# New instruction orders for all five engines of a two-layer attention kernel, weights requested by ScalarE, eight warm-up pairs

## Chip, core and metric

The kernel runs on one core of a Trainium2 chip. The metric is the device time of one execution in microseconds (us), as the median of several runs.

## What is computed

Two attention layers, one after the other, on x of shape (4, 128, 32, 32): four images, 128 channels, N = 1024 pixels. In each layer, for each image:

```
q = Wq x + bq     k = Wk x + bk     (16 x 1024 each)
v = Wv x + bv                       (128 x 1024)
energy = q^T k                      (1024 x 1024)
attn = softmax(energy, over keys)
x = gamma * (v attn^T) + x          (128 x 1024)
```

Everything is float32. Layer 1 works on the result of layer 0.

## The kernel before

There are eight stages, s = 0 to 7: stage s is layer s // 4 of image s % 4. Stages overlap. Each engine has its own instruction stream, and that stream is written out by hand: `PE_ORDER`, `ACT_ORDER`, `DVE_ORDER`, `POOL_ORDER` and `SP_ORDER` (lines 51 to 113) are lists of words such as `lo.6.3`: a kind of work, the stage, an index k or a half, and for TensorE's words a fourth number, the PSUM ring tile used. No planner runs; a program reads the words and emits the instructions, and semaphores are derived from the orders. Each engine takes its words strictly in order, so a word that waits holds all words behind it.

The kinds of work:

- `E` (TensorE): an energy tile, 128 queries by 1024 keys, into one of three ring tiles (two PSUM banks each). `max` (VectorE, line 563) takes its row maximum, `sum` (ScalarE, line 472) exponentiates and sums it. `log` (ScalarE) and `parts` (GpSimd, lines 391 to 396) turn maxima and sums into a shift for each query, in a high and a low part.
- `shift` (TensorE), `rows` (VectorE, line 572) and `place` (SyncE) put the shift into spare rows of the q and k operands.
- `ET` (TensorE): the transposed energies with the shift already in them. `attn` (ScalarE, line 484) exponentiates them into the SBUF tile attn.
- `hi` and `lo`: attn is split into a rounded high part (`hi`, line 359 on GpSimd, 490 on ScalarE) and the rest (`lo`: attn minus attn_hi, two SBUF inputs, line 364 on GpSimd, 558 on VectorE), so that TensorE can multiply both in its quick float32r mode. Of eight tiles of a stage, k = 1 to 6 are split; k = 0 and 7 are multiplied in plain float32. `v_hi` (370 on GpSimd, 495 on ScalarE) and `v_lo` (376 on GpSimd, 553 on VectorE) do the same for v.
- `PH` multiplies attn_hi by v_hi and v_lo (four passes), `PV` multiplies attn_lo by v_hi (two passes) or, for k = 0 and 7, the plain tiles. `finish` (VectorE, 581 and 586) forms gamma * out + x; `store` (SyncE) writes it out.
- `QX`, `QK` project q and k; `mask` and `stack` (VectorE, or GpSimd for stage 1 after `evac` on ScalarE) place them; `swap` (SyncE, line 323) copies the halves crosswise by DMA. `VX`, `V` and `v32` (line 548) make v. `raw` projects stage 0.
- `warm` is a number of matmul pairs on zeros; `WARM_UP` such pairs run first of all (lines 756, 757).

What holds buffers: `attn.s.k` may be written only when `lo.(s-1).k` has read the slot (for k = 0, 7: when `PV` has). `hi.s.k` needs the earlier stage's `PV` of that k. A ring tile is free when its reader is done. In the last two stages `PH` of each half of the output also waits for the `finish` of the same half of the stage before.

At the start SyncE issues, in this order, the DMAs of weights, of the two halves of image 0, of image 1, of `late` (v weights and layer 1), of units, and of images 2 and 3. ScalarE begins with the load of its activation table. The first `E` needs both halves of `qk_raw` (ScalarE, line 458) and, for tiles 0 to 3, the first half of `swapped_raw` (VectorE, line 519); for tiles 4 to 7 it needs both halves.

Of the kernel before, what the change touches and what calls it, by code (L numbers as in the profile page):

```python
# [77 lines left out]
attn.1.4 attn.1.6 log.2.1 attn.1.5 attn.1.7 attn.1.0 sum.3.0 hi.1.4 v_hi.2.0 sum.3.1 sum.3.2 attn.2.3 attn.2.1
attn.2.2 sum.3.6 sum.3.5 sum.3.4 sum.3.3 sum.3.7 attn.2.6 sum.4.4 log.3.1 attn.2.4 attn.2.5 attn.2.0 attn.2.7 hi.2.6
sum.4.0 sum.4.7 sum.4.1 sum.4.2 attn.3.3 attn.3.0 attn.3.1 attn.3.2 attn.3.4 sum.4.5 attn.3.6 sum.4.6 attn.3.5  # L80
hi.3.6 sum.4.3 log.4.1 sum.5.3 hi.3.5 sum.5.4 sum.5.6 sum.5.2 sum.5.1 attn.4.3 attn.4.2 attn.3.7 v_hi.4.0 attn.4.1
sum.5.7 sum.5.5 sum.5.0 attn.4.5 log.5.1 sum.6.6 attn.4.4 attn.4.0 attn.4.6 hi.4.4 sum.6.3 hi.4.6 hi.4.5 attn.4.7
# [6 lines left out]
max.0.6 max.0.0 max.0.7 max.0.4 max.0.2 max.0.1 max.0.3 max.0.5 max.1.4 rows.0.0 v32.0.0 max.1.7 max.1.6 mask.2.0
stack.2.0 max.1.5 max.1.0 max.1.2 rows.0.1 max.1.3 max.1.1 max.2.4 max.2.7 max.2.1 rows.1.1 v32.1.0 finish.0.0  # L90
max.2.3 max.2.0 mask.3.0 stack.3.0 max.2.6 max.2.2 max.2.5 finish.0.1 v32.2.0 lo.1.1 max.3.0 rows.2.1 max.3.1
max.3.2 mask.4.0 stack.4.0 finish.1.0 max.3.6 max.3.5 max.3.4 max.3.3 max.3.7 max.4.4 finish.1.1 v32.3.0 lo.2.2
# [1 line left out]
max.5.3 v32.4.0 max.5.4 rows.4.1 max.5.6 max.5.2 max.5.1 finish.3.0 mask.6.0 stack.6.0 max.5.7 max.5.5 max.5.0
max.6.6 finish.3.1 v32.5.0 max.6.3 rows.5.1 lo.4.2 max.6.2 mask.7.0 stack.7.0 finish.4.0 max.6.4 max.6.0 max.6.7
max.6.5 max.6.1 finish.4.1 max.7.0 max.7.4 max.7.1 rows.6.1 max.7.6 max.7.3 finish.5.0 max.7.2 v32.6.0 lo.5.4
max.7.7 v_lo.6.0 finish.5.1 max.7.5 v32.7.0 lo.6.5 rows.7.1 lo.6.6 lo.6.3 lo.6.4 finish.6.0 v_lo.7.0 lo.7.2
# [735 lines left out]
```

## Time and profile before

| | |
|---|---|
| median of 3 runs | 193.52 us (192.95 to 193.8) |
| the profiled execution's own time | 193.06 us |
| span of its profile | 191.3 us |
| TensorE busy | 179.1 us (94%) |
| VectorE busy | 145.7 us (76%) |
| ScalarE busy | 155.5 us (81%) |
| GpSimd busy | 156.9 us (82%) |

The span is the stretch from the first to the last record of the profile; the execution's own time has 1.8 us around it. TensorE's matmuls are pipelined and their ends are modelled, so its busy share says less than the distance between the starts of its instructions. In the rows below, PE is TensorE's matmul, PEld its weight load, DVE VectorE, ACT ScalarE, POOL GpSimd, SPq the DMA issues of SyncE.

### The profile page before, as it was taken

The page shows a single profiled execution, that of the slowest core. Times are in us where ns is not written, and L with a number is a line of the kernel's source. Part 1 is how long each engine was busy: PE and PEld are TensorE (multiplying, and loading weights), DVE is VectorE, ACT ScalarE, POOL GpSimd, SP SyncE. Part 2 cuts the span into 40 slices and gives each one's busy share as a digit, 9 for nine tenths or more (in the row PEclk, how much of TensorE's full clock was granted, in tenths as well). Part 3 has the DMA queues.
Part 4 walks back from the last instruction along what each step waited for, and adds up shares of the span by engine and source line. Part 5 has one row for each costly group of instructions (what it writes and reads, how often), then busy time and mean ns, then how long its engine had stood idle before and what let it go on. Part 6 is the DMA issues. An engine that isn't in the chain of part 4 may idle for free.

```text
span 191.3 us, 3482 instructions
## 1 busy us (share of the span) xinstructions
PE 179.1 (94%) x1282; PEld 123.1 (64%) x1282; DVE 145.7 (76%) x137; ACT 155.5 (81%) x223; POOL 156.9 (82%) x120
## 2 busy tenths in 40 slices
...
GB/s 155 345 104 0 215 9 42 69 3 3 2 113 0 5 111 3 0 3 3 110 3 0 3 55 58 2 3 107 61 55 7 55 0 58 3 0 55 55 55 55
DMA packets 3890, 9.51 MB, mean 50 GB/s; under 512 B 548, under 2 KB 932, under 8 KB 3876
## 3 DMA queue, kind: packets, MB, share of 16 engines
...
## 4 chain that ended last, share of the span: by engine, by line
PE 34%; POOL 31%; ACT 15%; issue 10%; DMA 4%; DVE 4%; SPq 1%; POOLq 0%; DVEq 0%; ACTq 0%
POOL attn_lo L364 14%; PE out_psum L720 10%; POOL attn_hi L359 9%; ACT ring L472 8%; PE out_psum L722 7%; ACT attn L484 4%; DMA qk_swapped<-qk 4%; PE ring L671 3%; PE ring L697 3%; PE out_psum L756 3%; PE ring L642 2%; DVE neg_max L563 2%; PE ring L624 2%; PE ring L657 2%; ACT attn_hi L490 2%
## 5 line engine op out<-in xcount | busy, mean ns | idle before, releaser
L364 POOL TENSOR_TENSOR attn_lo<-attn,attn_hi 128x1024 fp32r<-128x1024 f32 x37 | 90.4, 2455 | 1.8 <-ACT attn_hi L490 1.3
L563 DVE TENSOR_REDUCE neg_max<-ring 128x1 f32<-128x1024 f32 x64 | 75.6, 1219 | 15.7 <-PE ring L673 15.3
L472 ACT ACTIVATE ring<-ring,neg_max 128x1024 f32<-128x1024 f32 x64 | 69.6, 1087 | 9.9 <-DVE neg_max L563 9.3
L484 ACT ACTIVATE attn<-ring 128x1024 f32<-128x1024 f32 x64 | 63.3, 1024 | 9.8 <-DVE attn_lo L558 5.6
L359 POOL TENSOR_SCALAR attn_hi<-attn 128x1024 fp32r<-128x1024 f32 x35 | 39.2, 1134 | 5.5 <-ACT attn L484 5.4
L699 PE MATMUL ring<-qk_swapped,qk 64*128 64x512 f32 x64 | 29.0, 478 | 0.0
L697 PE MATMUL ring<-qk,qk_swapped 64*128 64x512 f32 x64 | 28.5, 468 | 0.3
L671 PE MATMUL ring<-qk_swapped,qk 64*128 64x512 f32 x56 | 25.1, 452 | 3.4 <-ACT attn L484 1.7
L673 PE MATMUL ring<-qk,qk_swapped 64*128 64x512 f32 x56 | 25.7, 461 | 0.0
L558 DVE TENSOR_TENSOR attn_lo<-attn,attn_hi 128x1024 fp32r<-128x1024 f32 x11 | 19.4, 1778 | 5.5 <-POOL attn_hi L359 4.7
L723 PE MATMUL out_psum<-attn_hi,v_hi 64*128 64x512 f32 x72 | 23.0, 399 | 0.0
L722 PE MATMUL out_psum<-attn_hi,v_hi 64*128 64x512 f32 x72 | 23.0, 398 | 0.0
L723 PE MATMUL out_psum<-attn,v 64*128 64x512 f32 x48 | 22.6, 590 | 0.0
L722 PE MATMUL out_psum<-attn,v 64*128 64x512 f32 x48 | 22.6, 590 | 0.0
L722 PE MATMUL out_psum<-attn_hi,v_lo 64*128 64x512 f32 x72 | 22.2, 388 | 0.0
L723 PE MATMUL out_psum<-attn_hi,v_lo 64*128 64x512 f32 x72 | 22.2, 388 | 0.0
L722 PE MATMUL out_psum<-attn_lo,v_hi 64*128 64x512 f32 x72 | 20.9, 392 | 0.1
L723 PE MATMUL out_psum<-attn_lo,v_hi 64*128 64x512 f32 x72 | 20.9, 392 | 0.0
L697 PEld LDWEIGHTS ring<-qk,qk_swapped 64*128 64x128 f32 x64 | 11.5, 184 | 10.9 <-issue 9.9
L657 PEld LDWEIGHTS ring<-late,x_all 64*128 64x128 f32 x256 | 16.6, 187 | 2.5 <-issue 1.7
L671 PEld LDWEIGHTS ring<-qk_swapped,qk 64*128 64x128 f32 x56 | 10.3, 184 | 12.3 <-issue 10.3
L657 PE MATMUL ring<-late,x_all 64*128 64x128 f32 x256 | 17.6, 275 | 0.2 <-ACT ring L472 0.2
...
## 6 DMA issues: line engine op xcount, KB each, us to landing
...
qk<-shift_rows SPq DMA_DIRECT2D x7, 8.0 KB
```

The source lines that it names most:

```text
L359: nc.gpsimd.tensor_scalar(attn_hi[:, k - 1], attn[:, k], 1.0, 0.0, ALU.mult, ALU.add).then_inc(cut_made["hi", "gpsimd"], 1)
L364: nc.gpsimd.tensor_tensor(attn_lo[:, k - 1], attn[:, k], attn_hi[:, k - 1].bitcast(fp32), ALU.subtract).then_inc(cut_made["lo", "gpsimd"], 1)
L472: nc.scalar.activation(e[:], e[:], ACT.Exp, bias=neg_max[s][:, i:i + 1], accum_out=row_sum[s][:, i:i + 1]).then_inc(sum_made, 1)
L484: nc.scalar.activation(attn[:, k], ring_tile("ET", s, k)[:].rearrange("p (a n) -> p a n", a=2), ACT.Exp).then_inc(attn_made, 1)
L563: nc.vector.tensor_reduce(neg_max[s][:, i:i + 1], ring_tile("E", s, i)[:], axis=AX.X, op=ALU.max, negate=True).then_inc(max_made, 1)
L657: last = nc.tensor.matmul(to[:, chunk], x_all[rows, s, chunk], late[rows, WV + layer(s)], start=step == 0 and j == 0, stop=step == 1 and j ...
L671: nc.tensor.matmul(to[:, 0:HALF], q_over_k[0:64, rows], k_over_q[0:64, 0:HALF], start=True, stop=True)
L673: nc.tensor.matmul(to[:, HALF:N], k_over_q[64:128, rows], q_over_k[64:128, HALF:N], start=True, stop=True).then_inc(e_mm, 1)
L697: nc.tensor.matmul(to[:, 0:HALF], k_over_q[0:64, first], q_over_k[0:64, part], start=True, stop=not added(s, h))
L699: last = nc.tensor.matmul(to[:, HALF:N], q_over_k[64:128, second], k_over_q[64:128, part], start=True, stop=not added(s, h))
L722: nc.tensor.matmul(out_psum[:, 0:HALF], v[0:64], a[0:64], start=start, stop=stop)
L723: last = nc.tensor.matmul(out_psum[:, HALF:N], v[64:128], a[64:128], start=start, stop=stop)
```

## The change

Three edits:

1. All five orders are replaced. The same set of tiles is computed. By kinds, the engines change so: GpSimd has 34 `hi` instead of 35, 33 `lo` instead of 37, 5 `v_hi` instead of 3, 4 `v_lo` instead of 5; VectorE has 15 `lo` instead of 11 and 4 `v_lo` instead of 3; ScalarE has 14 `hi` instead of 13 and 3 `v_hi` instead of 5. `warm` holds 19 pairs instead of 18. SyncE issues `swap.0.0` ahead of `swap.1.0`.
2. The DMA of the weights moves from the front of SyncE's queue to the front of ScalarE's, ahead of the table load.
3. `WARM_UP` is 8 instead of 10.

```diff
-WARM_UP = 10
+WARM_UP = 8
 PE_ORDER (its beginning)
-raw.0.0.0 raw.0.1.1 E.0.6.2 QX.1.0.0 E.0.0.1 QK.1.0.0 E.0.7.2 warm.0.2 E.0.4.0 E.0.2.1 E.0.1.2 warm.0.2 E.0.3.0
+raw.0.0.0 raw.0.1.1 warm.0.1 E.0.1.2 QX.1.0.0 E.0.2.1 QK.1.0.0 E.0.0.2 warm.0.2 E.0.7.0 E.0.3.1 E.0.5.2 warm.0.2
...
 PE_ORDER (its end)
-VX.7.0.2 E.7.5.0 ET.6.6.1 V.7.0.2 PH.6.1 PV.6.0
-ET.6.7.1 ET.6.3.2 shift.7.1.0 PH.6.6 PH.6.4 PH.6.5 PH.6.3 PH.6.2 ET.7.3.0 ET.7.2.2 PV.6.2 PV.6.1 PV.6.3 PV.6.6
-PV.6.5 PV.6.4 ET.7.0.1 ET.7.1.0 ET.7.6.2 PV.6.7 PH.7.2 ET.7.5.1 ET.7.4.0 ET.7.7.2 PV.7.2 PH.7.3 PV.7.0 PH.7.1 PH.7.6
-PV.7.1 PV.7.3 PH.7.5 PH.7.4 PV.7.6 PV.7.5 PV.7.4 PV.7.7
+VX.7.0.0 E.7.3.1 V.7.0.0 ET.6.5.2 PH.6.1
+PV.6.7 ET.6.0.0 ET.6.4.1 shift.7.1.2 PH.6.6 PV.6.1 PV.6.0 PV.6.6 PH.6.3 ET.7.7.2 ET.7.3.0 ET.7.2.1 PH.6.2 PV.6.3
+PV.6.2 PH.6.5 PH.6.4 ET.7.0.0 ET.7.4.1 ET.7.1.2 PV.6.4 PH.7.3 PV.6.5 ET.7.6.1 ET.7.5.0 PV.7.0 PH.7.1 PV.7.3 PH.7.2
+PH.7.5 PV.7.1 PV.7.2 PH.7.4 PH.7.6 PV.7.5 PV.7.4 PV.7.6 PV.7.7
 ACT_ORDER (its beginning and end)
-sum.0.6 evac.1.0 sum.0.0 sum.0.7 sum.0.4 sum.0.2 sum.0.1 sum.0.3 log.0.0 sum.0.5 sum.1.4 v_hi.0.0 log.0.1 sum.1.7
+sum.0.1 evac.1.0 sum.0.2 sum.0.0 sum.0.7 sum.0.3 sum.0.5 sum.0.4 log.0.0 sum.0.6 sum.1.0 sum.1.6 sum.1.7 log.0.1
...
-sum.7.5 log.7.1 hi.6.6 hi.6.4 attn.6.3 attn.6.7 attn.7.3 v_hi.7.0 attn.7.2 hi.7.2
-attn.7.0 attn.7.1 attn.7.6 attn.7.7 attn.7.5 attn.7.4 hi.7.5 hi.7.4
+sum.7.3 log.7.1 attn.6.5 v_hi.7.0 attn.6.0 attn.6.4 hi.6.3 hi.6.5 attn.7.3 attn.7.2 attn.7.7
+attn.7.4 attn.7.0 attn.7.1 attn.7.5 hi.7.5 hi.7.4 attn.7.6 hi.7.6
 DVE_ORDER (a piece of stages 2 to 4, and its end)
-lo.2.2
-rows.3.1 max.4.0 max.4.7 max.4.1 max.4.2 finish.2.0 mask.5.0 stack.5.0 max.4.5 max.4.6 v_lo.3.0 finish.2.1 max.4.3
+lo.2.2 rows.3.1
+lo.2.3 max.4.0 mask.5.0 max.4.6 stack.5.0 lo.2.6 finish.2.0 max.4.3 v_lo.3.0 max.4.4 max.4.1 max.4.7 max.5.5
...
-max.7.5 v32.7.0 lo.6.5 rows.7.1 lo.6.6 lo.6.3 lo.6.4 finish.6.0 v_lo.7.0 lo.7.2
-finish.6.1 lo.7.6 lo.7.5 finish.7.0 finish.7.1
+max.7.3 v32.7.0 lo.6.6 rows.7.1 lo.6.3 lo.6.5 lo.6.4
+finish.6.0 finish.6.1 lo.7.1 lo.7.2 lo.7.5 lo.7.4 finish.7.0 finish.7.1
 POOL_ORDER (its beginning and end)
-mask.1.0 stack.1.0 parts.0.0 parts.0.1 v_lo.0.0 hi.0.2 hi.0.3 hi.0.1 lo.0.2 lo.0.3 lo.0.1 parts.1.1 hi.0.6 lo.0.6
+mask.1.0 stack.1.0 parts.0.0 v_hi.0.0 v_lo.0.0 hi.0.2 parts.0.1 lo.0.2 hi.0.3 lo.0.3 hi.0.1 lo.0.1 parts.1.1
...
-parts.7.1 lo.6.2 hi.6.3 lo.6.1 hi.7.3 lo.7.3 hi.7.1 lo.7.1 hi.7.6
-lo.7.4
+parts.7.1 v_lo.7.0 hi.6.4 hi.7.3 hi.7.2 lo.7.3 hi.7.1 lo.7.6
 SP_ORDER
-swap.1.0 swap.0.0 place.0.0 swap.2.0
+swap.0.0 swap.1.0 place.0.0 swap.2.0
 the sync block
-            sp.dma_start(weights[:], weights_in).then_inc(weights_loaded, 16)
 the scalar block
+            act.dma_start(weights[:], weights_in).then_inc(weights_loaded, 16)
             act.preload_act_table_set("natural_log_exp_and_others")
```

## Rows read from the trace of the kernel before

**Rows 1.** The page: busy time and share of the span, by engine.
```profile
PE 179.1 (94%) x1282; PEld 123.1 (64%) x1282; DVE 145.7 (76%) x137; ACT 155.5 (81%) x223; POOL 156.9 (82%) x120
```

**Rows 2.** Busy us (and instructions) by stretch: PE, PEld, DVE, ACT, POOL; clock, DMA.
```profile
30.90:160.70 129.80, 125.50 (x1026) 94.77 (x1024) 110.45 (x109) 121.86 (x179) 125.04 (x88) 1.00 0.13 35
160.70:185.30 24.60, 23.40 (x98) 15.27 (x97) 16.45 (x12) 14.87 (x16) 20.00 (x12) 1.00 0.08 30
```

**Rows 3.** Timeline of the start: start us, us, engine, line, op [idle before, releaser].
```profile
0.74 0.39 SPq L310 DMA_DIRECT2D weights<-weights_in  x1
1.19 0.89 SPq L313 DMA_DIRECT2D x_all<-x_in  x2
...
4.27 0.63 PE L756 MATMUL out_psum<-zeros 64*128 64x512 bf16 x1
...
4.70 0.54 PE L756 MATMUL out_psum<-zeros 64*128 64x512 bf16 x1
...
5.38 3.70 PE L624 MATMUL ring<-x_all,weights 128*128 128x512 f32 x8
...
8.27 0.69 ACT L458 ACTIVATE qk_raw<-ring,weights 128x512 f32<-128x512 f32 x1 [0.96 <-PE ring L624]
...
9.12 0.75 DVE L519 TENSOR_SCALAR swapped_raw<-ring,weights 128x512 f32<-128x512 f32 x1 [0.89 <-PE ring L624]
...
10.02 0.66 PE L671 MATMUL ring<-swapped_raw,qk_raw 64*128 64x512 f32 x1 [0.94 <-DVE swapped_raw L519]
```

**Rows 4.** Line 310's and line 313's DMAs, from issue to landing.
```profile
DMA to landing us min/median/max: 2.2/2.2/2.2
...
DMA to landing us min/median/max: 2.7/3.0/3.3
```

**Rows 5.** Timeline of GpSimd: its first three attn_hi.
```profile
31.02 3.17 POOL L359 TENSOR_SCALAR attn_hi<-attn 128x1024 fp32r<-128x1024 f32 x3 [1.27 <-ACT attn L484]
```

**Rows 6.** Groups by line and form: count, busy us, mean ns, idle before them.
```profile
L364 POOL TENSOR_TENSOR attn_lo<-attn,attn_hi 128x1024 fp32r<-128x1024 f32 x37 | 90.4, 2455 | 1.8 <-ACT attn_hi L490 1.3
L359 POOL TENSOR_SCALAR attn_hi<-attn 128x1024 fp32r<-128x1024 f32 x35 | 39.2, 1134 | 5.5 <-ACT attn L484 5.4
L558 DVE TENSOR_TENSOR attn_lo<-attn,attn_hi 128x1024 fp32r<-128x1024 f32 x11 | 19.4, 1778 | 5.5 <-POOL attn_hi L359 4.7 <-ACT attn_hi L490 0.8
L376 POOL TENSOR_TENSOR v_lo<-v,v_hi 128x768 fp32r<-128x768 f32 x5 | 9.1, 1826 | 0.0
L553 DVE TENSOR_TENSOR v_lo<-v,v_hi 128x768 fp32r<-128x768 f32 x3 | 3.4, 1127 | 0.0
```

**Rows 7.** Timeline of GpSimd and VectorE around a `lo` on VectorE.
```profile
57.37 2.43 POOL L364 TENSOR_TENSOR attn_lo<-attn,attn_hi 128x1024 fp32r<-128x1024 f32 x1
...
59.04 1.84 DVE L558 TENSOR_TENSOR attn_lo<-attn,attn_hi 128x1024 fp32r<-128x1024 f32 x1
...
59.73 1.22 POOL L391 TENSOR_TENSOR shift<-neg_max,log_sum 128x8 f32<-128x8 f32 x1
```

**Rows 8.** Who waited for whom, whole span: us, times, longest us.
```profile
DVE neg_max L563 <- PE ring L673: 15.3, 20, 1.7
...
ACT ring L472 <- DVE neg_max L563: 9.3, 13, 3.5
```

**Rows 9.** Timelines of the end: TensorE after `V.7.0`, VectorE, GpSimd, ScalarE.
```profile
158.74 0.74 PE L720 MATMUL out_psum<-attn_hi,v_hi 128*128 128x512 f32 x2
...
162.66 2.84 DVE L558 TENSOR_TENSOR attn_lo<-attn,attn_hi 128x1024 fp32r<-128x1024 f32 x1
166.44 4.53 DVE L558 TENSOR_TENSOR attn_lo<-attn,attn_hi 128x1024 fp32r<-128x1024 f32 x2 [0.94 <-POOL attn_hi L359]
...
164.38 2.02 POOL L359 TENSOR_SCALAR attn_hi<-attn 128x1024 fp32r<-128x1024 f32 x1
...
169.93 1.03 ACT L484 ACTIVATE attn<-ring 128x1024 f32<-128x1024 f32 x1 [5.56 <-DVE attn_lo L558]
```

**Rows 10.** The chain that ended last: start us, us, what.
```profile
177.07 10.97 PE out_psum L720 x40
```

More of the change, by code:

```diff
@@ L78 @@
[L78 to L82, printed above, removed]
@@ new lines @@
+attn.0.2 attn.0.0 attn.0.3 sum.1.3 sum.1.2 attn.0.1 sum.1.5 sum.2.5 sum.1.1 sum.1.4 log.1.1 attn.0.4 sum.2.6
+attn.0.5 hi.0.5 attn.0.7 sum.2.2 attn.0.6 attn.1.2 attn.1.1 sum.2.4 sum.2.7 sum.2.0 attn.1.3 sum.2.1 sum.2.3 sum.3.0
+attn.1.6 attn.1.4 log.2.1 v_hi.2.0 attn.1.0 sum.3.7 sum.3.4 sum.3.3 attn.1.5 sum.3.2 attn.1.7 hi.1.5 attn.2.2
+attn.2.1 attn.2.3 sum.3.6 sum.3.5 sum.3.1 log.3.1 sum.4.2 attn.2.5 attn.2.4 attn.2.7 attn.2.6 hi.2.5 attn.2.0
+sum.4.0 attn.3.1 sum.4.6 attn.3.5 attn.3.2 attn.3.3 attn.3.0 sum.4.3 attn.3.4 sum.4.4 sum.4.1 sum.4.7 sum.5.5 hi.3.3
@@ new lines @@
+attn.3.6 sum.4.5 log.4.1 hi.3.4 sum.5.1 sum.5.4 attn.3.7 sum.5.7 sum.5.3 attn.4.6 attn.4.1 attn.4.3 attn.4.2
+attn.4.5 sum.5.6 sum.5.0 sum.5.2 sum.6.1 log.5.1 attn.4.0 attn.4.4 v_hi.5.0 attn.4.7 sum.6.3 sum.6.2 sum.6.0
+attn.5.3 hi.4.6 sum.6.6 attn.5.1 attn.5.2 attn.5.4 hi.5.2 sum.6.7 sum.6.5 sum.6.4 log.6.1 attn.5.0 attn.5.6 hi.5.4
+attn.5.5 sum.7.6 sum.7.0 sum.7.4 sum.7.2 attn.5.7 attn.6.2 sum.7.5 sum.7.7 attn.6.7 attn.6.1 sum.7.1 attn.6.3
+attn.6.6 hi.6.6 sum.7.3 log.7.1 attn.6.5 v_hi.7.0 attn.6.0 attn.6.4 hi.6.3 hi.6.5 attn.7.3 attn.7.2 attn.7.7
@@ L87 @@
+attn.7.4 attn.7.0 attn.7.1 attn.7.5 hi.7.5 hi.7.4 attn.7.6 hi.7.6
 """
 DVE_ORDER = """
[L89 to L92, printed above, removed]
@@ L93 @@
-rows.3.1 max.4.0 max.4.7 max.4.1 max.4.2 finish.2.0 mask.5.0 stack.5.0 max.4.5 max.4.6 v_lo.3.0 finish.2.1 max.4.3
[L94 to L97, printed above, removed]
@@ L98 @@
-finish.6.1 lo.7.6 lo.7.5 finish.7.0 finish.7.1
+max.0.1 max.0.2 max.0.0 max.0.7 max.0.3 max.0.5 max.0.4 max.0.6 max.1.0 rows.0.0 v32.0.0 max.1.6 max.1.7 mask.2.0
+stack.2.0 max.1.3 max.1.2 rows.0.1 max.1.5 max.2.5 max.1.1 max.1.4 max.2.6 v32.1.0 rows.1.1 finish.0.0 max.2.2
+mask.3.0 stack.3.0 max.2.4 max.2.7 max.2.0 max.2.1 max.2.3 max.3.0 finish.0.1 v32.2.0 lo.1.1 max.3.7 max.3.4 max.3.3
+rows.2.1 max.3.2 finish.1.0 mask.4.0 stack.4.0 max.3.6 max.3.5 max.3.1 max.4.2 finish.1.1 v32.3.0 lo.2.2 rows.3.1
@@ new lines @@
+lo.2.3 max.4.0 mask.5.0 max.4.6 stack.5.0 lo.2.6 finish.2.0 max.4.3 v_lo.3.0 max.4.4 max.4.1 max.4.7 max.5.5
+finish.2.1 max.4.5 v32.4.0 max.5.1 max.5.4 rows.4.1 max.5.7 max.5.3 finish.3.0 mask.6.0 stack.6.0 v_lo.4.0 max.5.6
+max.5.0 max.5.2 max.6.1 finish.3.1 lo.4.1 v32.5.0 rows.5.1 max.6.3 max.6.2 max.6.0 v_lo.5.0 max.6.6 finish.4.0
+mask.7.0 stack.7.0 max.6.7 max.6.5 max.6.4 finish.4.1 rows.6.1 v32.6.0 max.7.6 max.7.0 max.7.4 max.7.2 finish.5.0
+max.7.5 max.7.7 max.7.1 lo.6.2 lo.5.6 v_lo.6.0 finish.5.1 max.7.3 v32.7.0 lo.6.6 rows.7.1 lo.6.3 lo.6.5 lo.6.4
@@ L105 @@
-parts.5.1 lo.4.1 v_hi.5.0 lo.4.6 lo.4.5 hi.5.1 hi.5.2 lo.4.4 hi.5.3 v_lo.5.0 lo.5.3 parts.6.1 lo.5.1 lo.5.2 hi.5.4
-hi.5.5 hi.5.6 lo.5.5 lo.5.6 hi.6.2 hi.6.1 hi.6.5 parts.7.1 lo.6.2 hi.6.3 lo.6.1 hi.7.3 lo.7.3 hi.7.1 lo.7.1 hi.7.6
-lo.7.4
+mask.1.0 stack.1.0 parts.0.0 v_hi.0.0 v_lo.0.0 hi.0.2 parts.0.1 lo.0.2 hi.0.3 lo.0.3 hi.0.1 lo.0.1 parts.1.1
+v_hi.1.0 hi.0.4 lo.0.4 lo.0.5 hi.0.6 hi.1.2 lo.0.6 hi.1.1 v_lo.1.0 hi.1.3 lo.1.2 parts.2.1 lo.1.3 hi.1.6 hi.1.4
+lo.1.6 lo.1.4 v_lo.2.0 lo.1.5 hi.2.1 hi.2.2 parts.3.1 lo.2.1 hi.2.3 v_hi.3.0 lo.2.5 hi.2.6 hi.2.4 lo.2.4 hi.3.1
```

47 lines of the change are left out of this document (21 added, 26 removed).

## The prediction

> **What bounds the kernel now.** I read the page's busy shares first. No engine is idle enough to ignore: TensorE 94%, GpSimd 82%, ScalarE 81%, VectorE 76% [rows 1]. Such shares are averages, so I cut the span into three parts by the busy time of each stretch. Before 30.9 us GpSimd has nearly nothing to split, and the start is a chain of single steps. From 30.9 to 160.7 us GpSimd is busy 125.04 of 129.8 us, TensorE's modelled 125.50, ScalarE 121.86, VectorE 110.45 [rows 2]; the middle is balanced, with GpSimd the fullest engine and 4.76 us of it idle. After 160.7 us the split of the last two stages is left, and GpSimd is busy 20.00 of 24.6 us though VectorE helps [rows 2]. The chain of waits ends in 10.97 us of TensorE's products [rows 10], one `finish` and one store.
>
> The timelines show how the two engines disturb each other. A `lo` on VectorE starts at 59.04 us while GpSimd's own `lo` runs until 57.37 + 2.43 = 59.80 us; VectorE ends at 60.88, so it worked about 1.1 us and waited 0.7. GpSimd's next instruction, eight elements for each partition, takes 1.22 us instead of the 0.2 that its like takes elsewhere [rows 7]. So two-input work on VectorE and GpSimd's work take turns: it costs VectorE the rest of GpSimd's instruction, and GpSimd about 1.0 to 1.2 us.
>
> **The start.** Edits 2 and 3 act here. TensorE's warm pairs start 0.43 us apart up to the ninth, at 4.70 us [rows 3]: a matmul of 512 columns in 0.43 us is the 1.2 GHz level. The `raw` matmuls that follow at 5.38 us are 3.70 us for eight records, 0.43 apart; each is half of a four-pass float32 matmul, so this is 2.4 GHz. With eight pairs `raw` can begin where the ninth pair did, at 4.70: 0.68 us earlier. I charge 0.15 us for its first part at the lower level, since the ninth pair still ran there. Do the inputs come in time? Weights are requested at 0.74 and land 2.2 us later, at 2.94; the halves of image 0 are requested in 1.19 to 2.08 and land after 2.7 and 3.3, about 3.9 and 4.9 [rows 3, 4]. With the weights on the other queue the halves go one issue (0.45) earlier, 3.4 and 4.5, and the second half is needed only 1.7 us into `raw`. A request on ScalarE's queue is nowhere in this trace; its bounds are nothing and, as SyncE's first, 0.39 us of the queue plus a table load later by as much. ScalarE has no other work until the first `qk_raw`, so both ends cost nothing.
>
> Then the order. The first `E` was tile 6, which needs both halves of `swapped_raw`, ready at 9.12 + 0.75 = 9.87; it started at 10.02 [rows 3]. Now it is tile 1, which needs `qk_raw` (8.27 + 0.69 = 8.96) and one half; it stands behind `raw` (about 9.1) and one warm pair (0.2), so about 9.3 on the old clock. Gain 0.7, and 0.5 of the earlier `raw`: 1.2 us. `QK.1` stands behind the same number of `E` and `QX` words as before, so `evac.1`, `mask`, `stack` and the swap all move by the same 1.2 us. `swap.0.0`, now first, is ready at about 12 us and is out of SyncE's way before `swap.1.0`, so that reversal costs nothing; were it late, its two issues of 0.6 us would stand before `swap.1.0`. GpSimd's first `hi` at 31.02 waited for ScalarE's `attn` [rows 5]. In the new order ScalarE does the same three `sum` of stage 1 ahead of `attn.0.2` (3 in each) and no `v_hi`; I keep 1.2 less 0.1. On GpSimd, however, `parts.0.1` (three small instructions, about 0.7 us) now stands inside its full stretch. So what reaches the middle lies between 0.4 and 1.2; I take 0.8 us.
>
> **The middle.** From the first `hi` to `parts.7.1` I count words in both orders. GpSimd loses one `hi` (1.1), one `lo` (2.4), two `v_lo` (3.6) and gains one `v_hi` (no row of its own here; three quarters of a `hi` in width, 0.8) and one `parts` (0.7): 5.6 us less. VectorE gains three `lo` and two `v_lo`, five more turns at 1.0 to 1.2 us, 5.5 us that GpSimd stands still [rows 6, 7]. The two cancel: 0.1 us. ScalarE loses two `v_hi` and one `attn` and gains one `hi`, about 1.5 us less at some 1 us each. VectorE gets busier by 3 x 1.78 + 2 x 1.13 = 7.6 us [rows 6], from 110.45 to 118 of 129.8; the cover is its 19 us of idle time, mostly its waits for `E` (15.3 us over the span [rows 8]). So the middle's sum is nothing by load. Bounds: from a gain of half of GpSimd's 4.76 us idle (2.4) to a loss of 7.6, if VectorE's added time holds up the `max` behind it. I take 0, which the cancelling rows give.
>
> **The end.** Here the same exchange pays. Before, behind `parts.7.1`, GpSimd has 5 `lo` and 4 `hi`: 5 x 2.4 + 4 x 1.06 = 16.2 us without stalls [rows 5, 7]; VectorE has 7 `lo` and a `v_lo`, of which one `lo` lies before the stretch, 7 turns of 1.15 = 8.1: 24.3 of 24.6 us in which one of the two held the turn. Now GpSimd has 2 `lo`, 4 `hi` and a `v_lo`: 4.8 + 4.2 + 1.8 = 10.8; VectorE 8 `lo`: 9.2. Together 20.0: 4.3 us less. What that did is to be seen: VectorE's `lo.6.6` takes 2.84 us beside a `lo` of GpSimd; `hi.6.3` on GpSimd then takes 2.02 instead of 1.05; `lo.6.3` again waits for `lo.6.1`, until 169.83; and `attn.7.3`, which may overwrite that slot only then, starts at 169.93 after 5.56 us of idle ScalarE [rows 9]. In the new order `hi.6.3` is ScalarE's, behind three `attn`, a `v_hi` and nothing of GpSimd: on the old clock GpSimd's stretch begins at 160.7, right behind `log.7.1`, and 3 x 1.0 + 0.8 + 1.0 more is 165.5; `lo.6.3` follows by 167.9 even if it takes 2.4 us, 2.0 us earlier than 169.9. TensorE sets how much counts. From 158.74 to 188.04 (177.07 + 10.97) are 29.3 us [rows 9, 10]. Its words there are 12 `PH` (48 records), 12 split `PV` (24), 4 plain `PV` (16) and 10 `ET`: the last 40 records are 8 plain ones at 0.43 and 32 others, (10.97 - 3.44) / 32 = 0.235 each [rows 10]. 72 x 0.235 + 16 x 0.43 + 10 x 0.25 = 26.3 us. So 3.0 us are waits, and the new order has one more `ET`: the gain lies between 0 and 2.8. I take 2.0, what `attn.7.3` comes earlier, and not the upper end, since the other waits are not accounted for.
>
> The rows say that a `lo` holds the turn for 2.4 us on GpSimd and for 1.0 to 1.2 us on VectorE [rows 7]. The Trainium skill (Perfetto Trace Analysis, "Optimizing Scalar/DVE Operations") speaks against the exchange: as the two engines share a read port of SBUF, moving work between them might not help. By the rows the sum is 190.3 us; by that rule alone the end would give nothing and the sum would be 192.3. The trace agrees that they exclude each other, and not that the exchange is worthless, since the two prices differ.
>
> **Sum.** 193.06 (profiled execution) - 0.8 - 0 - 2.0 = 190.3 us. The median of the runs lies 0.46 above that execution, which I take as half noise: 190.5 us.
>
> **Rivals.**
> *The exchange brings nothing at the end* (15%). A `lo` moved to VectorE still stops GpSimd, the tail stays as full, and only the start counts: 193.52 - 0.8 = 192.7 us. For it: `lo.6.6` took 2.84 us on VectorE, more than GpSimd's 2.4 [rows 6, 9]. Against: all but 1.1 of that was waiting. The rule cited under the end describes this case.
> *VectorE becomes late* (11%), the slower side. In the middle the five added instructions (`lo.2.3`, `lo.2.6` and others) stand ahead of `max` words; a late `max` holds `sum`, the ring tile and the next `E`. Its price is up to 7.6 us; it decides the case once more than 2.8 of these, 37%, reach TensorE. At 60%, 4.6: 193.5 - 2.8 + 4.6 = 195.3 us. For it: VectorE's mean `lo` is 1.78 us, and each waits unseen behind GpSimd. Against: its 19 us of idle time.
> *The middle gains too* (22%). Turns that fall when GpSimd is at a boundary cost VectorE less, and GpSimd's idle time shrinks by half: 2.4, with 0.8 and the full 2.8: 193.5 - 6.0 = 187.5 us.
> *The clock stays low* (2%). If eight pairs don't bring the 2.4 GHz level, `raw` takes 3.7 us more, and with 2.8 gained the time is 194.4.
>
> **Numbers.** My forecast has 50%. What this kernel's measurement can tell from no change is about 0.5%, 1.0 us: faster means under 192.55, slower over 194.5. Faster: 50% + 22% + 3% of the first rival = 75%. The same 14% are the rest of the first rival and the low clock, slower 11% the late VectorE. The range of 8 in 10 is 187.2 to 193.8: it takes in the case of the gaining middle and the start alone, and leaves out the slower side.
>
> **What would show it.** Start: `raw` at about 4.7, first `E` at about 8.8, first `attn_hi` of GpSimd near 30. Middle: VectorE busy about 7 us more, GpSimd's last `parts` about 1 us earlier than 160.79. End: ScalarE's 5.56 us wait for `attn_lo` is under 3, GpSimd is busy under 14 us behind `parts.7.1`, and TensorE needs about 27 us from the end of `V.7.0`. The prediction is wrong if ScalarE's wait for VectorE's `max` (9.3 us in all before [rows 8]) grows by several us, or if the gap in the tail only moves to another word.

## The result, and the profile after

| | before | after |
|---|---|---|
| median of the runs, us | 193.24 (4 runs) | 196.63 (4 runs: 195.72, 195.87, 197.4, 197.94) |
| profiled execution, us | 193.06 | 195.72 |
| its span, us | 191.3 | 193.9 |

The ratio is 1.0178, with an interval of 1.0136 to 1.0219. The kernel became 3.4 us slower where 3 us less were forecast, and its time lies above the range. Here is the page of the kernel after: busy time and share by engine. (Line numbers after are lower by one or two than those of before.)

```profile
PE 180.2 (93%) x1280; PEld 123.4 (64%) x1280; DVE 148.1 (76%) x142; ACT 156.5 (81%) x222; POOL 145.1 (75%) x116
```

GpSimd lost 11.8 us of busy time against [rows 1], and the kernel is slower all the same. The next fence cuts the span at the same events as [rows 2]: GpSimd's first `hi` (30.1), `parts.7.1` (165.0) and the last products. Each row has the busy us of TensorE, its weight load, VectorE, ScalarE and GpSimd.

```profile
30.10:165.00 134.90, 127.22 (x1030) 95.17 (x1026) 118.27 (x114) 122.85 (x178) 120.62 (x88) 1.00 0.12 33
165.00:187.90 22.90, 22.35 (x96) 15.12 (x96) 11.36 (x12) 15.97 (x17) 12.33 (x10) 1.00 0.08 31
```

The middle is 134.9 us long; it was 129.8. VectorE's load in it is 118.27, and I had forecast 118. GpSimd's idle time in it grew from 4.8 to 14.3 us. So VectorE's load came out as it was added up, and the time did not follow it. GpSimd's load did not come out. I had counted 5.6 us less of its own work and 5.5 us more of standing still; its busy time in the middle fell by 4.4 us, so only about 1.2 us of standing still can be seen in it. Over the span GpSimd now waits 10.4 us for ScalarE's `attn` (5.4 before) and 5.6 for ScalarE's `hi` (1.3 before), and it is no longer the fullest engine of the middle. By form, the groups that answer to [rows 6] (count | busy us, mean ns | idle before them) are these.

```profile
L362 POOL TENSOR_TENSOR attn_lo<-attn,attn_hi 128x1024 fp32r<-128x1024 f32 x33 | 81.0, 2465 | 6.4 <-ACT attn_hi L489 5.6
L557 DVE TENSOR_TENSOR attn_lo<-attn,attn_hi 128x1024 fp32r<-128x1024 f32 x15 | 18.8, 1288 | 3.5 <-ACT attn_hi L489 2.3 <-POOL attn_hi L357 1.0
L552 DVE TENSOR_TENSOR v_lo<-v,v_hi 128x768 fp32r<-128x768 f32 x4 | 6.6, 1642 | 0.0
```

A `lo` on VectorE became shorter in the mean, 1.29 us for 1.78, and nearly all of that is at the end (2.06 to 1.22 us; 1.44 to 1.35 in the middle). A `v_lo` became longer, 1.64 for 1.13.

TensorE shows where the time went. I took the starts of its records and added up what lies between two starts beyond the usual spacing of the first. That sum is 25.6 us before and 28.0 after, 2.4 more, which nearly covers the longer span (2.6 us).

| TensorE's waits, us | before | after | `turns_back` | `edits_tail` |
|---|---|---|---|---|
| to 31 us | 9.0 | 8.4 | 8.4 | 8.9 |
| 31 to 160 us | 13.1 | 16.7 | 15.6 | 12.8 |
| from 160 us | 3.5 | 2.9 | 2.8 | 2.5 |
| span | 191.3 | 193.9 | 192.7 | 189.9 |

(The last two columns are experiments, told below.) The start won 0.6, the end 0.6, and the middle lost 3.6. Three long waits in the middle stand out. The first: VectorE's timeline around 129 us, with GpSimd's row and TensorE's beside it.

```profile
128.51 7.77 POOL L362 TENSOR_TENSOR attn_lo<-attn,attn_hi 128x1024 fp32r<-128x1024 f32 x3
...
129.26 2.44 DVE L552 TENSOR_TENSOR v_lo<-v,v_hi 128x768 fp32r<-128x768 f32 x1
...
131.62 1.21 DVE L562 TENSOR_REDUCE neg_max<-ring 128x1 f32<-128x1024 f32 x1
132.76 0.74 DVE L580 SCALAR_TENSOR_TENSOR x_all<-out_psum,weights,x_all 128x512 f32<-128x512 f32 x1
...
134.38 0.47 PE L721 MATMUL out_psum<-attn_hi,v_hi 64*128 64x512 f32 x1 [1.29 <-issue]
```

`v_lo.5.0` is one of the words that moved to VectorE. It started while GpSimd was 0.75 us into a `lo`, and took 2.44 us. Behind it stood a `max` and then `finish.4.0`, two instructions; they free the output for `PH.4.5`, which started 0.1 us after the second one ended (133.53 + 0.75). The profile names no releaser for this wait. In the experiment `vlo_ahead` it names `finish` for the like one. The other two are the swaps of stages 4 and 6, on the chain of waits and in TensorE's timeline; the row at 35.31 is a shorter wait for the swap of stage 2.

```profile
71.66 5.07 DMA qk_swapped<-qk
114.06 5.07 DMA qk_swapped<-qk
```

```profile
35.31 0.50 PE L670 MATMUL ring<-qk_swapped,qk 64*128 64x512 f32 x1 [0.67 <-DMA qk_swapped<-qk]
...
76.77 0.50 PE L670 MATMUL ring<-qk_swapped,qk 64*128 64x512 f32 x1 [1.33 <-DMA qk_swapped<-qk]
...
119.17 0.50 PE L670 MATMUL ring<-qk_swapped,qk 64*128 64x512 f32 x1 [1.21 <-DMA qk_swapped<-qk]
```

TensorE came to the first `E.4` at 76.77 - 1.33 = 75.44 us, 4.4 us after the swap's first issue (71.08), and to the first `E.6` 4.5 us after its own (113.48). Before, there were 6.9 us at stage 4 (67.94 to 74.86), but at stage 6 only 4.3, so there the order left no more time than after. At stage 2 it came 3.6 us after the issue; before, 6.3. (The wait of 0.7 us there replaces one of the same length before, for ScalarE at 35.40.) From the first issue to the last landing the swaps of stages 4 and 6 took 5.65 us each; before, the same two took 4.4 and 4.5. In both long ones the records have a fetch of instructions (a 16 KB packet of the instruction queue, at 74.3 and 116.7), each 3.2 us behind the issue. Before, the fetch near stage 4 came at 74.0, after the landing, and the one at stage 6 came at 116.0, 3.7 us behind the issue and 0.8 ahead of the landing.

### The profile page after: what moved, and what is told of

Same layout as the page of the kernel before. It is cut to its first block, busy times and chain, and to the rows that moved or that the text cites. A ratio compares the mean times of both kernels' runs of the same rounds, so it can differ in the third digit from the quotient of the medians.

```text
span 193.9 us, 3478 instructions
## 1 busy us (share of the span) xinstructions
PE 180.2 (93%) x1280; PEld 123.4 (64%) x1280; DVE 148.1 (76%) x142; ACT 156.5 (81%) x222; POOL 145.1 (75%) x116
## 4 chain that ended last, share of the span: by engine, by line
PE 60%; DVE 12%; POOL 7%; DMA 7%; ACT 6%; issue 5%; SPq 1%; POOLq 0%; ACTq 0%
PE out_psum L721 17%; PE out_psum L719 11%; DMA qk_swapped<-qk 7%; PE ring L670 6%; PE ring L641 5%; PE ring L696 5%; PE ring L656 4%; ACT ring L471 4%; POOL attn_lo L362 4%; DVE neg_max L562 4%; PE out_psum L722 4%; PE out_psum L755 2%; PE ring L623 2%; DVE masked_hi L529 2%; DVE qk L536 2%
## 5 line engine op out<-in xcount | busy, mean ns | idle before, releaser
L562 DVE TENSOR_REDUCE neg_max<-ring 128x1 f32<-128x1024 f32 x64 | 75.8, 1219 | 13.5 <-PE ring L672 13.1
L362 POOL TENSOR_TENSOR attn_lo<-attn,attn_hi 128x1024 fp32r<-128x1024 f32 x33 | 81.0, 2465 | 6.4 <-ACT attn_hi L489 5.6
L471 ACT ACTIVATE ring<-ring,neg_max 128x1024 f32<-128x1024 f32 x64 | 69.6, 1088 | 11.0 <-DVE neg_max L562 10.3
L357 POOL TENSOR_SCALAR attn_hi<-attn 128x1024 fp32r<-128x1024 f32 x34 | 36.6, 1087 | 10.5 <-ACT attn L483 10.4
L670 PE MATMUL ring<-qk_swapped,qk 64*128 64x512 f32 x56 | 25.1, 448 | 4.6 <-DMA qk_swapped<-qk 3.2
L696 PE MATMUL ring<-qk,qk_swapped 64*128 64x512 f32 x64 | 27.5, 447 | 1.4 <-ACT attn L483 1.2
L698 PE MATMUL ring<-qk_swapped,qk 64*128 64x512 f32 x64 | 28.2, 458 | 0.0
L672 PE MATMUL ring<-qk,qk_swapped 64*128 64x512 f32 x56 | 25.5, 456 | 0.0
L721 PE MATMUL out_psum<-attn_hi,v_hi 64*128 64x512 f32 x72 | 23.2, 401 | 1.3 <-issue 1.3
L722 PE MATMUL out_psum<-attn_hi,v_hi 64*128 64x512 f32 x72 | 23.3, 403 | 0.0
L722 PE MATMUL out_psum<-attn_lo,v_hi 64*128 64x512 f32 x72 | 21.8, 396 | 0.0
L721 PE MATMUL out_psum<-attn_lo,v_hi 64*128 64x512 f32 x72 | 21.8, 396 | 0.0
L557 DVE TENSOR_TENSOR attn_lo<-attn,attn_hi 128x1024 fp32r<-128x1024 f32 x15 | 18.8, 1288 | 3.5 <-ACT attn_hi L489 2.3
L585 DVE SCALAR_TENSOR_TENSOR x_all<-out_psum,weights,x_all 128x512 f32<-128x512 f32 x16 | 12.0, 751 | 10.4 <-PE out_psum L719 10.0
L656 PEld LDWEIGHTS ring<-late,x_all 64*128 64x128 f32 x256 | 16.7, 187 | 2.7 <-issue 1.9
```

The lines of the kernel that those rows point to most:

```text
L357: nc.gpsimd.tensor_scalar(attn_hi[:, k - 1], attn[:, k], 1.0, 0.0, ALU.mult, ALU.add).then_inc(cut_made["hi", "gpsimd"], 1)
L362: nc.gpsimd.tensor_tensor(attn_lo[:, k - 1], attn[:, k], attn_hi[:, k - 1].bitcast(fp32), ALU.subtract).then_inc(cut_made["lo", "gpsimd"], 1)
L471: nc.scalar.activation(e[:], e[:], ACT.Exp, bias=neg_max[s][:, i:i + 1], accum_out=row_sum[s][:, i:i + 1]).then_inc(sum_made, 1)
L562: nc.vector.tensor_reduce(neg_max[s][:, i:i + 1], ring_tile("E", s, i)[:], axis=AX.X, op=ALU.max, negate=True).then_inc(max_made, 1)
L656: last = nc.tensor.matmul(to[:, chunk], x_all[rows, s, chunk], late[rows, WV + layer(s)], start=step == 0 and j == 0, stop=step == 1 and j ...
L670: nc.tensor.matmul(to[:, 0:HALF], q_over_k[0:64, rows], k_over_q[0:64, 0:HALF], start=True, stop=True)
```

## The experiments

A time of before stands beside each, from the same chip.

**`edits_only`**: the order of before with edits 2 and 3.

```diff
-WARM_UP = 10
+WARM_UP = 8
-            sp.dma_start(weights[:], weights_in).then_inc(weights_loaded, 16)
+            act.dma_start(weights[:], weights_in).then_inc(weights_loaded, 16)
```

> The kernel before with edits 2 and 3 alone (weights on ScalarE's queue, eight warm pairs), old orders. In the changed kernel's trace raw began 0.54 us earlier, at 4.84, but took 4.86 us instead of 3.70 because its first three records ran 0.7 to 1.0 us apart, and it ended later than before. Theory A (these edits cost a little: two warm pairs less let the 2.4 GHz level come later): raw ends near 9.7 instead of 9.1, total +0.3 to +0.8 us over the kernel before. Rival (the late rise was chance, the edits are worth 0.5 us as predicted): raw ends near 8.6, total -0.3 to -0.6. In either case they can't explain the 3.4 us that the change lost.

Measured 192.93 us against 193.29, ratio 0.9984 [0.9962, 1.0006]. `raw` starts at 4.50, and takes its 3.70 us as before:

```profile
4.50 3.70 PE L624 MATMUL ring<-x_all,weights 128*128 128x512 f32 x8
```

The rival of the expectation held: the late rise of the clock in after was not a fixed cost of the edits. They don't harm, and what they bring can't be told from nothing by this run alone.

**`orders_only`**: the other half, the new orders with ten pairs and the weights on SyncE's queue (the same lines as above, back from after).

> The changed kernel with edits 2 and 3 undone (weights on SyncE's queue, ten warm pairs), new orders. Theory A: the loss is in the orders; time 195.8 to 196.8 us, ratio to before 1.013 to 1.019, raw of 3.7 us. Rival (the start's edits cost most of it): ratio below 1.008. If the first E (tile 1) now starts at 9.3 instead of 10.02, the order's gain at the start (0.7) is real.

Measured 197.98 against 193.29, ratio 1.0239 [1.02, 1.0278]. So the orders are the whole loss. It is larger than I had expected (195.8 to 196.8 us), and the first `E` began at 9.90 us, not at 9.3. In its profile 5.9 us of TensorE's waits lie between 82 and 103 us (1.7 in the profile of after), 1.8 of them at `PH.2.6`, which waits for `finish.2.0`. The swaps of stages 4 and 6 took 4.3 and 4.4 us here, and TensorE hardly waited for them: the orders lose this much without the long transfers.

**`swap_slack`**: after, with the first energy tiles of stages 4 and 6 behind the v projection, so that the swaps have more time.

```diff
 PE_ORDER
-E.4.2.2 PV.1.5 VX.3.0.1
+PV.1.5 VX.3.0.1 E.4.2.2
-E.6.1.2 PV.3.4 VX.5.0.1
+PV.3.4 VX.5.0.1 E.6.1.2
```

> The changed kernel with E.4.2 moved behind VX.3.0 and E.6.1 behind VX.5.0 in TensorE's order, nothing else. Theory S: TensorE stood 1.5 and 1.4 us at these two words for a swap DMA that had 5.7 us between stack and E, where the old order left 6.9; the words behind them were ready. Then the waits of TensorE for qk_swapped fall by 2 to 3 us and the time falls by 1.5 to 2.8 us to about 194. Rival (TensorE only waits elsewhere, since ScalarE and VectorE also need these E early): the waits fall and the time stays within 0.5 us of 196.6.

Measured 194.66 against 193.29, ratio 1.0074 [1.0041, 1.0107]. TensorE's waits for the swaps all but went, but a wait for the same ring tile came up behind each, in the next `ET` on it:

```profile
79.66 0.47 PE L696 MATMUL ring<-qk,qk_swapped 64*128 64x512 f32 x1 [1.52 <-ACT ring L471]
```

Its ten executions lie in two groups, 194.1 to 195.0 and 196.2 to 196.75, and the profile is one of the second: its waits sum to 27.7 us, hardly fewer than after. So the medians say that the moves help by about 1%, and no profile shows how.

**`finish_first`**: after, with `v_lo.5.0` behind `finish.4.0`.

```diff
 DVE_ORDER
-v_lo.5.0 max.6.6 finish.4.0
+max.6.6 finish.4.0 v_lo.5.0
```

> The changed kernel with v_lo.5.0 moved behind finish.4.0 in VectorE's order, nothing else. In the changed kernel v_lo.5.0 took 2.44 us on VectorE (1.0 of its own, the rest waiting for GpSimd's lo), finish.4.0 behind it began 2 us after its products were ready, and PH.4.5, which waits for finish.4.0, left TensorE idle 1.3 to 1.5 us. Theory V (the rival of the prediction: VectorE late by its added turns, here through a finish): PH.4.5 starts about 1.3 us earlier and the time falls by 0.8 to 1.5 us. Rival (max.6.6 ahead of finish.4.0 holds it anyway until 132.8): no more than 0.3 us is gained, and v_lo.5.0 only waits later.

Measured 196.24 against 193.29, ratio 1.0152 [1.0107, 1.0197]. A miss: the wait of 1.5 us at `PH.4.5` is gone, but the median fell by 0.4 us and not by 0.8 to 1.5. In this profile `PH.2.6` waits, as in `orders_only`. Here are VectorE and GpSimd around 88 us, first of after, then of `finish_first`.

```profile
88.90 1.22 DVE L557 TENSOR_TENSOR attn_lo<-attn,attn_hi 128x1024 fp32r<-128x1024 f32 x1
...
89.06 3.30 POOL L362 TENSOR_TENSOR attn_lo<-attn,attn_hi 128x1024 fp32r<-128x1024 f32 x1
...
90.20 0.75 DVE L580 SCALAR_TENSOR_TENSOR x_all<-out_psum,weights,x_all 128x512 f32<-128x512 f32 x1
```

```profile
88.14 2.39 POOL L362 TENSOR_TENSOR attn_lo<-attn,attn_hi 128x1024 fp32r<-128x1024 f32 x1
...
88.31 3.31 DVE L557 TENSOR_TENSOR attn_lo<-attn,attn_hi 128x1024 fp32r<-128x1024 f32 x1
91.54 0.74 DVE L580 SCALAR_TENSOR_TENSOR x_all<-out_psum,weights,x_all 128x512 f32<-128x512 f32 x1
...
93.17 0.47 PE L721 MATMUL out_psum<-attn_hi,v_hi 64*128 64x512 f32 x1 [1.66 <-DVE x_all L585]
```

Whoever starts first has the turn. In after VectorE's `lo.2.6` came 0.16 us ahead of GpSimd's `lo.2.4` and took 1.22 us, and GpSimd paid (3.30). In `finish_first` it came 0.17 us behind, took 3.31, and `finish.2.0` and with it TensorE paid 1.66 us. That could be the reason for after's two groups of times, some 1.8 us apart. It is argued from three profiles, and the next run, made to test it, did not bear it out.

**`lo_behind_finish`**: after, with that `lo.2.6` directly behind `finish.2.0`.

```diff
 DVE_ORDER
-stack.5.0 lo.2.6 finish.2.0
+stack.5.0 finish.2.0 lo.2.6
```

> The changed kernel with lo.2.6 moved behind finish.2.0 in VectorE's order, nothing else. The executions of the changed kernel fall in two groups, 195.7 to 195.9 and 197.4 to 197.9 us, and three profiles of the new orders show both: in one, lo.2.6 started 0.16 us ahead of GpSimd's lo.2.4 and took 1.22 us; in another, 0.17 us behind it and took 3.30 us, finish.2.0 began at 91.5 instead of 90.2 and PH.2.6 left TensorE idle 1.9 us. Theory R (who takes the turn first decides, through the finish behind it): with finish.2.0 ahead, the slow group goes and the time is 195.0 to 195.9 in all executions. Rival (the groups have another cause, such as a DMA): the two groups stay, median within 0.4 of 196.6.

Measured 197.35 against 193.68, ratio 1.019 [1.0145, 1.0234]. A miss: all four executions (196.44 to 198.1 us) lie above the 195.0 to 195.9 expected, so what makes the two groups stays open. `PH.2.6`'s wait went, and 1.0 us came up at `E.4.1` (94.4) and 1.7 at `E.5.5` (98.4). The `lo` now stood in front of `max.4.3`. That the two new waits come from there is argued, not tested.

**`swap_deep`**: after, with the same two tiles put one `ET` further back than in `swap_slack`, and their `max` and `sum` moved along (stage 4 is shown; stage 6 is done alike).

```diff
 PE_ORDER
-E.4.2.2 PV.1.5 VX.3.0.1 ET.2.5.0 V.3.0.1 ET.2.4.2
+PV.1.5 VX.3.0.1 ET.2.5.0 V.3.0.1 ET.2.4.2 E.4.2.2
 DVE_ORDER
-max.4.2 finish.1.1 v32.3.0
+finish.1.1 v32.3.0 max.4.2
```

> The changed kernel with E.4.2 behind ET.2.4 and E.6.1 behind ET.4.4, their max and sum moved likewise. In the kernel with slack (E.4.2 behind VX.3.0) TensorE's 1.5 us gap only moved to ET.2.4.2, which needs the same ring tile as E.4.2. Theory S2: the gap goes when the ring's order changes too; TensorE's waits for the swap fall under 1 us, and the time is 2.0 to 2.8 us below the changed kernel, 193.8 to 194.6. Rival (TensorE's order there is balanced with ScalarE's, which now lacks two sums early): log.4.1 and log.6.1 come no earlier, and the gain is under 0.8 us.

Measured 195.92 against 193.68, ratio 1.0122 [1.0088, 1.0155]. A miss (193.8 to 194.6 expected), and worse than `swap_slack`: `E.4.2` now waits 1.4 us for its ring tile, which `attn.2.4` frees at 78.57.

**`vlo_ahead`** turns the question round: it is the kernel before, with one word taken from GpSimd to VectorE, at the place that it has in after. **`vlo_behind`** is the same with that word one place later.

```diff
 POOL_ORDER
-v_lo.5.0
 DVE_ORDER (vlo_ahead)
-stack.7.0 finish.4.0 max.6.4
+stack.7.0 v_lo.5.0 finish.4.0 max.6.4
 DVE_ORDER (vlo_behind)
+stack.7.0 finish.4.0 v_lo.5.0 max.6.4
```

> The kernel before with one part of the exchange alone: v_lo.5.0 taken from GpSimd (where it took 1.80 us at 136.0) and put on VectorE directly ahead of finish.4.0, about where the new order has it. My prediction priced this at nothing, since GpSimd saves 1.8 and VectorE has idle time. Theory V (it delays the finish behind it by its own 1.0 us and by what is left of GpSimd's instruction): finish.4.0 starts 1 to 3 us later than 129.36, TensorE waits for it, and the time rises by 0.5 to 1.5 us, to about 194.3. Rival (load counts, not place): the time falls or stays, 192.6 to 193.4.

> The kernel before with v_lo.5.0 on VectorE as well, but directly behind finish.4.0. The same load as the kernel with it ahead of finish.4.0; only the place differs. Theory V (the place decides): no loss, 192.6 to 193.5 us, 0.5 to 1.5 us under the kernel with it ahead. Rival (load on VectorE decides): both kernels have the same time within 0.3 us.

Measured 196.0 (ratio 1.0113 [1.0078, 1.0149]) and 194.63 (1.0053 [1.0036, 1.007]) against 193.68. By the ratios one `v_lo` on VectorE costs 2.2 us ahead of `finish` and 1.0 behind it, though GpSimd has less to do. The first half of what was expected held, with more loss than the 0.5 to 1.5 us forecast: the place is worth 1.2 us. The second, no loss behind `finish`, was a miss: 1.0 us remains, and no run separates where it comes from. The chain of waits of `vlo_ahead` is plain, and below it is TensorE's row.

```profile
127.79 1.28 DVE qk L536
129.07 2.14 DVE v_lo L552
131.21 0.67 DVE x_all L580
...
131.91 0.76 DVE x_all L585
...
132.76 0.46 PE out_psum L721
```

```profile
132.76 0.46 PE L721 MATMUL out_psum<-attn_hi,v_hi 64*128 64x512 f32 x1 [1.75 <-DVE x_all L585]
```

**`turns_back`** tests several words together: after, with four words of the middle back on GpSimd. **`turns_back_slack`** adds the moves of `swap_slack`.

```diff
 DVE_ORDER
-lo.2.3 lo.2.6 v_lo.4.0 v_lo.5.0
 POOL_ORDER
-hi.2.3 v_hi.3.0 lo.2.5 hi.2.6
+hi.2.3 lo.2.3 v_hi.3.0 lo.2.5 hi.2.6 lo.2.6
-v_hi.4.0
+v_hi.4.0 v_lo.4.0
-hi.5.3
+hi.5.3 v_lo.5.0
```

> The changed kernel with four of VectorE's added turns given back to GpSimd: lo.2.3, lo.2.6, v_lo.4.0, v_lo.5.0. GpSimd gets 2 x 2.4 + 2 x 1.8 = 8.4 us more of its own and about 4.3 fewer of standing still, in a middle in which it was busy 130 of 155 us; VectorE gets about 7 us less. Theory V (VectorE's late words, above all the finish words behind the turns, cost the middle): PH.4.5's gap of 1.5 us and the slow group go, median 194.2 to 195.4 against 196.6. Rival G (GpSimd then becomes late, as the exchange was meant to prevent): 196.5 to 199.

> The last kernel and the moved E.4.2 and E.6.1 (behind VX.3.0 and VX.5.0), which alone took 2.0 us off the changed kernel. If the two causes are separate (turns on VectorE, words placed before their swap has landed), the gains add: 192.5 to 194.0 us, near the kernel before. Rival: they share their slack, and this has the time of the better one, 194.2 to 194.9.

`turns_back` measured 194.44 against 193.72, ratio 1.0039 [1.0012, 1.0066]; after had 1.0178. By these ratios the four words cost 1.0178 - 1.0039, 1.4% or 2.7 us (from both intervals I estimate 1.7 to 3.7, after having only four runs). The time is in the range that theory V gave. The row of its windows that answers to the middle (its profiled execution took 195.29 us, near the longest of the ten):

```profile
30.10:163.80 133.70, 128.05 (x1030) 96.47 (x1026) 113.31 (x110) 122.47 (x177) 126.84 (x93) 1.00 0.12 34
```

VectorE has 5.0 us less than after and GpSimd 6.2 more, and the stretch is 1.2 us shorter. `PH.4.5` has no wait, and the swap of stage 6 (now 4.42 us) delays nobody.

But the middle is not mended. From GpSimd's first `hi` to the start of `V.7.0` it takes 126.7 us before (126.6 in `edits_only`), 130.9 after and 129.7 here, and TensorE's waits in it are 15.6 us where before has 13.1. `edits_tail` below, with the old middle and much the same gains at start and end, is 1.0039 - 0.9914, 1.25% or 2.4 us faster than `turns_back`. So an estimated 2.4 us of the middle's loss are left when the four words are back. One wait of 1.3 us, at 96.3 for ScalarE's `attn`, is new here; what causes it and the rest was not tested.

`turns_back_slack` measured 196.28, ratio 1.0128 [1.0084, 1.0173]. That was a miss: the two gains don't add. The ring-tile waits of `swap_slack` are there again (1.7 us at 79.4, 1.5 at 123.6), while the waits for swaps that they bought off had mostly gone by themselves.

**`tail_exchange`** does only the end of the exchange, in the orders of before. **`edits_tail`** adds edits 2 and 3.

```diff
 POOL_ORDER
-parts.7.1 lo.6.2 hi.6.3 lo.6.1 hi.7.3
+parts.7.1 lo.6.2 hi.7.3
 DVE_ORDER
-lo.6.6 lo.6.3
+lo.6.6 lo.6.1 lo.6.3
 ACT_ORDER
-attn.6.3 attn.6.7 attn.7.3
+attn.6.3 attn.6.7 hi.6.3 attn.7.3
```

> The kernel before with the exchange of the end alone: hi.6.3 from GpSimd to ScalarE behind attn.6.7, lo.6.1 from GpSimd to VectorE behind lo.6.6. My prediction gave 2.0 us to this (ScalarE waited 5.56 us for lo.6.3). In the changed kernel the stretch from V.7.0 to the last finish took 30.4 us against 31.1. Theory A (TensorE's own work bounds the end): the wait of ScalarE falls under 3 us and the time by 0.5 to 1.0 us, to about 192.8. Rival (prediction): 191.7 or less. Rival (nothing): within 0.3 us of the kernel before.

> The kernel before with the end's exchange and with edits 2 and 3 (weights on ScalarE's queue, eight warm pairs), a candidate for a version faster than both. Edits alone measured 0.9984 of before. If both parts hold and add, 0.3 + 0.7 = 1.0 us: ratio 0.993 to 0.996. If the end gives nothing, 0.998.

Measured 192.81 (0.9958 [0.9929, 0.9987]) and 192.16 (0.9914 [0.9878, 0.995]) against 193.72. The second did a little better than expected (0.993 to 0.996) and beats both kernels: before by 1.6 us and, by the two ratios, after by 5. ScalarE's row in `tail_exchange` answers to the 5.56 us of [rows 9]:

```profile
168.58 1.03 ACT L483 ACTIVATE attn<-ring 128x1024 f32<-128x1024 f32 x1 [2.69 <-PE ring L698]
```

`attn.7.3` no longer waits for a `lo`, but for its own `ET`, and TensorE's waits from 160 us fall from 3.5 to about 2.5 us.

## Why the prediction was wrong

**The middle is the step that failed.** I priced it at nothing "by load": VectorE's 7.6 us had a "cover", its 19 us of idle time. VectorE's load was right (118.27 us), the cover was not. VectorE takes its words in order, and its idle time lay in other places than the added words: before, it waited for `E` tiles between `max` words [rows 8], after, it still does so for 13.1 us.

```profile
DVE neg_max L562 <- PE ring L672: 13.1, 19, 2.0
...
ACT ring L471 <- DVE neg_max L562: 10.3, 11, 2.6
```

The words were put where VectorE had no idle time, in front of `finish.4.0` and `finish.2.0`, and there a late start costs TensorE at once. `vlo_ahead` against `vlo_behind` shows it with one word (1.2 us for the place), and `turns_back` shows that four of the added words, priced at nothing, cost about 2.7 us together. That is about half of what the middle lost by the medians (by the profiles 1.2 of 4.2 us); some 2.4 us more stay open. What is shown is the rival that I gave 11%, *VectorE becomes late*. Its price, 4.6 us, came near the middle's loss (4.2 us in the profiles), but only half of that is shown to be VectorE's, so the nearness of its 195.3 us to the measured 196.63 is in part luck. But I had it act through a late `max`, and watched ScalarE's wait for `max`, which grew by only 1.0 us (9.3 to 10.3). Where one wait could be isolated, it acted through `finish`. In stages 0 to 5 both halves of the output use the whole of `out_psum`, so the first product of the second half (k = 4 to 7) waits for the `finish` of the first half of the same stage: `PH.4.5` for `finish.4.0`, `PH.2.6` for `finish.2.0`. My account of the kernel names only the like waits of the last two stages, and I followed none of them. `finish` isn't all of it either: taking one of these waits out of after gained 0.4 us (`finish_first`) or nothing (`lo_behind_finish`), since others came up behind.

The price of a turn on VectorE was too low at these places. I took 1.0 to 1.2 us from [rows 7]. That is the work; a word that arrives second waits for the rest of GpSimd's instruction too. `v_lo.5.0` took 2.44 us in after, and `lo.2.6` 3.31 in `finish_first`, 2.2 of them waiting. In [rows 7] itself it was 1.84. GpSimd's side was priced too high: of 5.5 us of standing still about 1.2 can be seen.

**I didn't cost the swaps.** The time from a swap's issue until TensorE comes to the first tile that needs it shrank from 6.9 to 4.4 us at stage 4 and from 6.3 to 3.6 at stage 2, and no step of mine looked at it. The usual transfer takes 4.3 us, so nothing was left in hand, and each longer transfer is a wait of TensorE. (Stage 6 had no more in hand before; there the transfer itself was longer.) That these waits cost about 1% is suggested by `swap_slack`. `turns_back_slack` contradicts it, and `orders_only` lost more without them, so their own share stays open.

**The end was right in kind and too large in size.** GpSimd is busy 12.33 us from `parts.7.1` on (under 14 forecast), and `attn.7.3` idles ScalarE for 1.84 us, and not for a `lo` (under 3 forecast). Instead of 2.0 us it brought 0.6 to 0.7: TensorE's waits there fell from 3.5 to 2.9, and from the start of `V.7.0` to the last `finish` it took 30.4 us instead of 31.1. `tail_exchange` gives 0.8 in the orders of before. My count of turns there had a slip: it left out the one `lo` of VectorE that lies ahead of the stretch before, but not the one after (7 `lo` follow `parts.7.1`, not 8); the term of 2.0 us didn't rest on it. Two things were missing in that term. `attn.7.3` was bound by `ET.7.3` next (ScalarE waits 1.84 us for it, 2.69 in `tail_exchange`), and TensorE's own words filled the rest. And `max.7.3`, the last `max`, came 0.9 us later behind `V.7.0` than the last `max` did before; two `lo`, `v_lo.6.0` and `finish.5.1` stand right in front of it:

```profile
156.15 2.97 DVE L557 TENSOR_TENSOR attn_lo<-attn,attn_hi 128x1024 fp32r<-128x1024 f32 x2
159.05 1.80 DVE L552 TENSOR_TENSOR v_lo<-v,v_hi 128x768 fp32r<-128x768 f32 x1
160.77 0.74 DVE L580 SCALAR_TENSOR_TENSOR x_all<-out_psum,weights,x_all 128x512 f32<-128x512 f32 x1
161.54 0.75 DVE L585 SCALAR_TENSOR_TENSOR x_all<-out_psum,weights,x_all 128x512 f32<-128x512 f32 x1
162.21 1.22 DVE L562 TENSOR_REDUCE neg_max<-ring 128x1 f32<-128x1024 f32 x1
```

The page of the Trainium skill that I weighed there (Perfetto Trace Analysis, "Optimizing Scalar/DVE Operations") says that moving work between the two engines might not help. In the end of the kernel it did help, by `tail_exchange`; in the middle it did harm, and not only nothing. The rule is a warning that holds by place.

**The start came to the forecast 0.8 us, by another way.** GpSimd's first `hi` began at 30.23 instead of 31.02:

```profile
30.23 1.05 POOL L357 TENSOR_SCALAR attn_hi<-attn 128x1024 fp32r<-128x1024 f32 x1 [1.78 <-ACT attn L483]
```

But I had `raw` at 4.7 for 3.85 us and the first `E` at 8.8. In the profile after they are these:

```profile
4.84 4.86 PE L623 MATMUL ring<-x_all,weights 128*128 128x512 f32 x8
...
9.86 0.59 PE L670 MATMUL ring<-swapped_raw,qk_raw 64*128 64x512 f32 x1
```

`raw` waited 0.14 us for the weights, which landed at 4.5 (0.73 + 3.8) and not near 2.9, and then took 1.16 us longer than in [rows 3], with its first records 0.7 to 1.0 us apart. The first `E` is 0.16 us earlier, not 1.2. The rest came from the order behind it: from the first `E` to the first `hi` are 20.4 us in after and in `orders_only`, and 21.0 before and in `edits_only`. That the start came to 0.8 is luck in part. In `lo_behind_finish`, which starts by the same words as after, `raw` took 3.81 us, the first `E` began at 8.81 as forecast, and the first `hi` at 29.17, 1.85 us earlier than before.

**Which rivals fell.** *The middle gains too* had the sign wrong. *The exchange brings nothing at the end* is excluded by `tail_exchange`, just (0.9929 to 0.9987). *The clock stays low* didn't happen as I had it, but in part, below.
